# A four-block transformer layer on one core: a finer order of the attention's side work, one shared-expert batch earlier, and a mixture-of-experts dispatch by a table

## The reference

```
x = x + transformer_block(layernorm(x), ctx)   # masked self-attention, LN, cross-attention on ctx, LN, FFN 256-1024-256 (ReLU), LN
x = x + int8_matmul(layernorm(x))              # each row scaled by its amax/127, rounded, times int8 weights
x = x + attention(layernorm(x), ctx, ctx)      # cross-attention, no mask
h = layernorm(x)
logits = h @ router.T ; top 2 of 16 experts, gate = sigmoid(logit)
x = x + sum_k gate_k * down[e_k](silu(gate[e_k](h)) * up[e_k](h)) + shared_down(silu(shared_gate(h)) * shared_up(h))
```

## Time and profile before

| | us |
|---|---|
| median of 3 timed runs | 1551.65 (1545.44 to 1557.75) |
| the profiled execution | 1535.08 |
| its span, first to last instruction | 1533.3 |
| TensorE busy in it | 1291.2 (84%) |
| VectorE busy | 929.4 (61%) |
| ScalarE busy | 671.0 (44%) |
| Pool busy | 466.3 (30%) |

### The profile page before, as it was taken

One profiled execution on the slowest core, in us unless ns is written; L12 is line 12 of the kernel. 1 busy time (PEld: TensorE's weight loads), 2 busy tenths in 40 slices (PEclk: granted clock), 3 DMA queues, 4 the chain that ended last, 5 costly groups with the idle time before them and its releaser, 6 DMA issues. The chain is left out here.

```text
span 1533.3 us, 17810 instructions
## 1 busy us (share of the span) xinstructions
PE 1291.2 (84%) x5544; PEld 562.0 (37%) x5544; DVE 929.4 (61%) x2123; ACT 671.0 (44%) x1243; POOL 466.3 (30%) x728
## 2 busy tenths in 40 slices
PE   5787878878788889988988988988889848999991
PEld 2221322322323233443442443443333224656661
DVE  5799989899885665456455555558667322233333
ACT  1255545455454556445445545535546521112220
POOL 4341633322212323243343343232301004413341
PEclk9598988999899999989999988998989678999996
DMA  7642422424432542221221221222331129722225
GB/s 229 197 131 71 130 77 76 131 56 147 119 92 86 138 125 56 91 69 35 83 77 35 83 76 35 83 68 85 104 89 37 43 73 353 243 71 84 79 64 165
DMA packets 130703, 156.69 MB, mean 102 GB/s; under 512 B 15534, under 2 KB 106162, under 8 KB 130355
## 3 DMA queue, kind: packets, MB, share of 16 engines
q1 hardware_dynamic: 118067, 134.53, 30.0%
q10 hardware_dynamic: 8704, 12.58, 2.6%
q0 software_dynamic: 3840, 8.43, 1.5%
HBM read 93.92 MB, written 63.05 MB: 102 GB/s over the span
## 5 line engine op out<-in xcount | busy, mean ns | idle before, releaser
L1077 DVE TENSOR_REDUCE Mx<-bank 128x1 f32<-128x512 f32 x512 | 341.3, 685 | 304.7 <-PE bank L843 301.4
L750 ACT ACTIVATE prob<-bank 128x512 f32<-128x512 f32 x512 | 290.0, 593 | 253.5 <-PE bank L860 251.8
L860 PE MATMUL bank<-QS,KS 99*128 99x512 bf16 x768 | 315.1, 412 | 68.1 <-ACT prob L750 29.9
L843 PE MATMUL bank<-KS,QS 96*128 96x512 bf16 x768 | 319.2, 416 | 60.1 <-DVE Mx L1074 29.8
L750 ACT ACTIVATE prob<-prob 128x512 f32<-128x512 f32 x256 | 160.6, 629 | 178.5 <-DVE prob L1088 176.8
L873 PE MATMUL bank<-prob,V 128*17 128x512 f32 x1536 | 227.6, 668 | 0.7 <-ACT prob L750 0.7
L860 PEld LDWEIGHTS bank<-QS,KS 99*128 99x128 bf16 x768 | 76.1, 100 | 296.8 <-ACT prob L750 140.2
L843 PEld LDWEIGHTS bank<-KS,QS 96*128 96x128 bf16 x768 | 77.0, 100 | 282.1 <-DVE Mx L1074 104.8
L597 POOL TENSOR_SCALAR MR<-neg 16x128 bf16<-16x128 f32 x48 | 13.8, 288 | 318.5 <-ACT neg L724 318.4
L1088 DVE TENSOR_TENSOR prob<-bank,ff_h 128x512 f32<-128x512 f32 x128 | 87.5, 684 | 16.7 <-PE bank L860 16.3
L1088 DVE TENSOR_TENSOR prob<-bank,mask 128x512 f32<-128x512 f32 x128 | 87.7, 685 | 13.0 <-PE bank L860 12.8
(11 more groups left out here) (157 smaller groups left out, 1727.9 us busy)
## 6 DMA issues: line engine op xcount, KB each, us to landing
stack_scr<-parts SPq DMA_DIRECT2D x48, 384.0 KB, 2.6
QS<-stack_scr SPq DMA_DIRECT2D x48, 384.0 KB, 4.1
KS<-stack_scr SPq DMA_DIRECT2D x48, 384.0 KB, 5.0
stack_scr<-parts SPq DMA_DIRECT2D x48, 256.0 KB, 2.9
w_gu<-in_gate_up ACTq DMA_DIRECT2D x16, 512.0 KB, 5.5
disp<-zero SPq DMA_DIRECT2D x2, 3096.0 KB, 15.4
xr<-disp SPq DMA_DIRECT2D x48, 129.0 KB, 2.0
stack_scr<-parts SPq DMA_DIRECT2D x48, 128.0 KB, 2.8
```

Source lines behind the costliest of these rows:

```text
L750: act.activation(prob[:, U % NP_, j, :], src, ACT.Exp, scale=CAST).then_inc(exp_done, 1)
L843: pe.matmul(bankS[i % NS][:, :], QS[0:STACK, v, qt * P:(qt + 1) * P], KS[0:STACK, v, :], start=True, stop=True).then_inc(s_full, 1)
L860: pe.matmul(bankT[e % NT][:, :], KS[0:ROWS, h, kt * P:(kt + 1) * P], QS[0:ROWS, h, :], start=True, stop=True).then_inc(t_full, 1)
L1077: dve.tensor_reduce(dst, b, AX.X, ALU.max).then_inc(s_read, 1)
```

## The change

1. `batch_order()`: a third list, `at`, is keyed by quarters (`place(step, ...)` takes fractions of a step). Nearly all side work of attentions 4 to 11 moves to it. ScalarE's reading gets names of its own (`head`, `hT`, `aT`, `relu`), placed a quarter step or so behind the product; `turn` and `attT` are single halves, `apply` single rows (`quarters`), `ff2` pieces of four of eight k blocks, `norm` single rows. `oT` and its reading (`merge`) stand at quarters 1 and 3 of the step. The second half of k and q and the values go from five steps ahead of their attention to around its start. The sum of x and the normed rows goes from Pool (`norm`) to VectorE (`stats` 4).
2. The shared expert of batch 0 (`gate`, `up`, `swish`, `hid`, `down`, `sadd`) is done behind the last attention, in phase one (EARLY_SHARED = 1); the shared weights are loaded in phase one, into the mask's place.
3. `acc` (which R now is), `identf` and the transposed rows of batches 1 to 3 stay on chip between the phases; `x_scr`, `tT_scr`, `route_scr` and `disp` go.
4. Dispatch: in place of rows, a pair (row number, gate) is scattered to `tag_scr`, which has 2048 places per expert and is filled with NOWHERE before. 24 such scatters run on Pool in phase one (`dispatch`), 8 at the start of phase two. One gather then reads the 48 tiles' pairs into `table`, TensorE turns it, VectorE makes addresses (`addresses`), and Pool gathers the rows of each tile from `t_scr` by an indirect DMA.
5. Expert weights are issued by SP at the start of phase two; the last reads of `y_tok` (now k-major) are shared between SP and ScalarE.

```diff
+    def place(step, *ops, apart=0):
+        for i, op in enumerate(ops):
+            at.setdefault(round(HG * step) + apart * i, []).append(op)
+    def column(step, n, what, m, lag=0.5):
+        place(step, ("col", n, what, m))
+        place(step + 0.25, ("head", n, what, m))
+        place(step + lag, ("cut", n, what, m))
+    def turned(step, p, i):
+        place(step, *halves("turn", p, i), apart=1)
+        place(step + 0.25, *halves("hT", p, i), apart=1)
+    def attended(e, n, i):
+        p = n % B
+        place(e - 0.5, *halves("attT", n), apart=1)
+        place(e - 0.25, *halves("aT", n), apart=1)
+        place(e + 0.25, *halves("out", n), apart=2)
+        place(e + 0.75, *halves("add", n), apart=2)
+        place(e + 1.5, *halves("stats", p, i), apart=1)
+        place(e + 2.25, *quarters("apply", p, i), apart=1)
...
-            put(late, e, ("attT", n - B), *halves("out", n - B))
-            put(early, e + 1, *halves("add", n - B), *halves("stats", p, a))
-            put(early, e + 2, *halves("apply", p, a), *halves("affine", p, a))
-            put(late, e + 4, ("turn", p, a), *halves("res", p, a))
...
+            attended(e, n - B, a)
+            place(e + 3.75, *halves("affine", p, a), apart=1)
+            turned(e + 5.25, p, a)
+            place(e + 5.75, *halves("res", p, a), apart=1)
+            place(first - 11, ("ctx", n))
+            column(first - 8.75, n, "k", 0)
+            column(first - 6.75, n, "q", 0)
+            column(first - 1.75, n, "k", 1, 1.5)
+            column(first + 0.75, n, "q", 1, 0.75)
...
+                for i, step in enumerate((1, 1.5, 2.25, 2.75, 3.25, 3.75, 4.25, 4.75)):
+                    place(f + step, ("ff1", p, i))
+                    place(f + step + 0.25, ("relu", p, i))
+                for i, step in enumerate((5.75, 6.25, 6.75, 7.75, 8.25, 8.75, 9.25, 9.75)):
+                    place(f + step, ("ff2", p, i // 4, i // 2 % 2, i % 2))
...
+            attended(e, n, 6)
+            turned(e + 3.25, p, 6)
+            place(e + 4.25, ("logits", p))
+            place(e + 4.5, ("top", p))
+            place(e + 5, ("rank", p))
+            place(e + 5.25, ("route", p))
+            if n < NB - 1:
+                for t in range(QT):
+                    place(e + 6.5 + t, ("dispatch", p, t))
+            else:
+                for m, step in enumerate((1, 2.25, 4.5, 5.5)):
+                    place(e + step, ("gate", 0, m), ("up", 0, m))
+                for m, step in enumerate((1.5, 3, 5, 6)):
+                    place(e + step, ("swish", 0, m))
...
+                    place(e + 6.25 + half / 2, ("down", 0, half, 0), ("down", 0, half, 1))
...
             order += between[len(between) * j // HG:len(between) * (j + 1) // HG]
+            order += at.get(HG * step + j, [])
...
-                for half in range(2):
-                    t, x_half = T[p][:, 2 * half:2 * half + 2, :], R[p][:, 2 * half:2 * half + 2, :]
...
-                        pool.tensor_tensor(x_half, x_half, t, ALU.add).then_inc(norm_ready, 1)
...
+                def dispatch(p, t):
+                    pool.wait_ge(route_ready[p], 1)
+                    pool.wait_ge(blanked, 16)
+                    for k in range(2):
+                        pool.indirect_dma_start(tag_scr, bass.IndirectOffsetOnAxis(slot[:, p * QT + t, k:k + 1], 0),
+                                                tags[:, p * QT + t, k, :], None).then_inc(tagged, 16)
...
-                for t in (2 * half, 2 * half + 1):
-                    ins = act.activation(dst[:, t, :], src[:, t, :], ACT.Identity,
...
+                    if i == 4:
+                        link(dve.tensor_tensor(R[p][:, rows, :], R[p][:, rows, :], T[p][:, rows, :], ALU.add))
...
+                def rows(s):
+                    if s >= NX:
+                        pool.wait_ge(xT_full, s - NX + 1)
+                    pool.indirect_dma_start(xr[:, s % NX, :], None, tokens_of,
+                                            bass.IndirectOffsetOnAxis(token[:, s:s + 1], 0)).then_inc(xr_in[s % NX], 16)
+                for s in range(NX):
+                    rows(s)
                 for s in range(TILES):
...
+                    if s + NX < TILES:
+                        rows(s + NX)
...
+                for t in range(1, TT, 2):
+                    act.dma_start(got[:, t % NR, :, :], y[t]).then_inc(got_in[t % NR], 16)
...
+                        if n == 2 * QT - 1:
+                            pe.wait_ge(token_ready, 1)
...
+                        if c == 1 and m == 1:
+                            turn_table()
```

More of the change, by code:

```diff
@@ L90, in batch_order @@
             for half in range(2):
[L91 to L109 removed]
+                step = (s + 3 if p == 0 else first - 5) + half
@@ L110, in batch_order @@
             for half in range(2):
-                put(late, first - 5 + half, ("v", n, half))
-                put(early, first - 4 + half, ("val", n, half))
+                place(first - 0.25 + 1.5 * half, ("v", n, half))
+                place(first + 0.25 + 1.5 * half, ("val", n, half))
             if a == 2:
[L114 to L117, removed]
@@ new lines, in batch_order @@
+                for i, step in enumerate((5.75, 6.25, 6.75, 7.75, 8.25, 8.75, 9.25, 9.75)):
+                    place(f + step, ("ff2", p, i // 4, i // 2 % 2, i % 2))
+                place(f + 8.25, ("ffadd", p, 0))
+                place(f + 10.25, ("ffadd", p, 1), ("again", p))
+                place(f + 10.5, *halves("stats", p, 3), apart=1)
+                place(f + 11.5, *quarters("apply", p, 3), apart=1)
+                for t, step in enumerate((12.5, 13, 13.25, 13.5)):
+                    place(f + step, ("norm", p, t))
@@ L135, in batch_order @@
+                place(f + 19.5, ("i8", p))
+                place(f + 20, *halves("i8add", p), apart=1)
+                place(f + 20.5, *halves("stats", p, 5), apart=1)
+                place(f + 21.5, *quarters("apply", p, 5), apart=1)
+                turned(f + 22.5, p, 5)
+                place(f + 23, *halves("res", p, 5), apart=1)
         for g in range(NG):
             if n or g >= 2:
-                s = first - 1
+                s = first - (2 if n else 1)
                 if n:
@@ L186, in jobs_made @@
 def jobs_made(kind, *at):
[L188 to L191 removed]
     if kind == "i8":
         return [(kind, *at, half) for half in range(2)]
[L194 removed]
+    if kind in ("turn", "attT", "col", "v", "out", "ff1", "i8T", "logits", "rank", "gate", "up"):
         return [(kind, *at)]
[L196 to L200 removed]
+    if kind in ("ff2", "down"):
+        return [(kind, *at[0:2])] if not any(at[2:]) else []
+    if kind in ("max", "oT"):
+        return [(kind, *at)]
     return []
 def jobs_read(kind, *at):
[L206 to L207 removed]
+    read_by_act = {"hT": "turn", "aT": "attT", "relu": "ff1", "swish": "gate"}
+    if kind in read_by_act:
+        return "act", jobs_made(read_by_act[kind], *at)
     made = {"val": "v", "cut": "col", "i8turned": "i8T", "top": "logits", "route": "rank"}
@@ L940, in _ @@
                         read_done(pe, ("ff1", p, FT - 1))
-                        tokens(("ff2", *at[0:2]), at[1], ff_h, w_ff2, FT, (at[2],))
+                        tokens(("ff2", *at[0:2]), at[1], ff_h, w_ff2, FT, (at[2],),
+                               range(FT // 2 * at[3], FT // 2 * (at[3] + 1)))
+                    elif kind in ("gate", "up"):
+                        read_done(pe, ("turn", p, NORMS - 1, KD - 1))
+                        if at == [0, 0]:
+                            pe.wait_ge(shared_in, 48)
+                        columns((kind, *at), s_gu[:, ("gate", "up").index(kind), :, :], hT[p], at[1])
+                    elif kind == "down":
+                        read_done(pe, ("up", p, HT - 1))
+                        tokens(("down", *at[0:2]), at[1], hid[p], s_dn, HT, (at[2],))
                     elif kind == "i8T":
```

553 lines of the change are left out of this document (280 added, 273 removed).

## The result

The changed kernel takes 1483.2 us (median of 4 runs, 1478.0 to 1486.7) beside 1549.6 us before: ratio 0.956, 95% interval 0.951 to 0.962. The forecast was 1479. The total is right; several terms in it are not, and two of them only appear in the experiments.

The account below looks back on a forecast made before the run. VectorE was taken to bound the masked attentions and TensorE the eight unmasked ones. Order -48, masked stretch -4, tail and shared expert -22, dispatch +1 sum to -73 us: 1551.65 - 73 = 1479 us, range 1435 to 1535.

Parts of the forecast that it names:

- Order, -48: Unmasked attentions: the quarter-step order saves 48 us: 8 from filled steps, 20 of waits, 20 of clock.
- rival (a): Attentions: the order gives nothing, waits move to VectorE's maxima or root and apply; 1531 us, chance 0.13.
- Readers come a quarter step behind their product, so most of the 29.9 us should go.: Unmasked attentions: with ScalarE's readers later, TensorE's 29.9 us of waits for exponentials shrink by two thirds, 20 us.
- Late columns, 0: Second half of k and q and values nearer their attention: nothing; a few us per batch if SP's queue is held.
- Masked stretch, -4: Masked attentions, bound by VectorE: the finer order of the next attentions' norms and projections saves 4 us (0 to 15).
- Tail and shared expert, -22: Behind the last attention: one batch's shared expert fills TensorE's idle time in the tail, saving 22 us (15 to 25).
- Dispatch, +1: Start of phase two: table of places by small scatters and a gather is tight, costing 1 us (0 to 5).
- Loop, 0: Expert loop: tiles stay at TensorE's 3.02 us, Pool's scatter and gather needing 2.6 us; no change, little room.
- (c): Expert loop: each Pool issue waits for one VectorE operation, 3.3 us a tile, 14 us more, 1493 us; chance 0.04.
- (d): Expert loop: scatters land late behind gathers in Pool's one queue; 1533 us, or 1591 us at worst; chance 0.08.
- (e): Second phase: weights or table not in time, saved shared work becomes a wait; up to +20 us, 1499 us; chance 0.04.
- rival (b): Attentions: the order recovers 95 us; 1432 us, chance 0.09.

Follow-up runs that it names:

- e1: Changed kernel with the step order of the kernel before for all attentions; tail, table and on-chip data stay: 1525.7 us, ratio 0.984.
- e7: Changed kernel with ScalarE's readers (column heads, ReLUs, copies of turned rows) back in their product's quarter: 1446.8 us, ratio 0.937.
- e8: Changed kernel with k and q of the second half and the values placed ahead of the attention again: 1512.0 us, ratio 0.980.
- e12: e10 with VectorE's readers sooner: every cut a quarter behind its product, each value a quarter sooner: 1488.0 us, ratio 0.963.
- e5: Changed kernel with the turn of the normalised inputs of batches 1 to 3, and their columns, one step later: 1474.4 us, ratio 0.952.
- e13: Changed kernel with only the copies of turned rows back in their product's quarter; ReLUs and column heads stay later: 1451.6 us, ratio 0.943.
- e10: Changed kernel with the edits of e7 and e5 together: 1446.8 us, ratio 0.936.
- e2: Changed kernel with the shared expert of all four batches in the second phase, none in the tail: 1498.2 us, ratio 0.966.
- e9: Changed kernel with each row gather of the expert loop issued twice, the second into an unread buffer: 1509.4 us, ratio 0.979.
- e3: Changed kernel with the loads of the shared expert's weights issued 27 steps later: 1484.7 us, ratio 0.958.
- e6: e5 with the tag scatters of the first batch four steps later: 1473.3 us, ratio 0.953.
- e11: e10 with each batch's eight tag scatters in one piece right behind a load of the rows MR: 1449.7 us, ratio 0.938.

## Why the prediction came out right, point by point

- **Order, -48.** Measured 43 us (e1), inside its bounds, but made of other parts. I had 20 us of waits, 20 of clock and 8 of filled steps. In the unmasked stretch it is 36 us of clock and 7 of idle. My reason for the clock was that long stalls become shorter. Counted in the timelines of TensorE, it idled for more than 2 us seven times in this stretch before, eleven times in e1 and three times in the changed kernel, with nearly the same idle time in all; that fits, but no run separates it from the rest. One reading under it was off: the window at clock 0.51 stands ahead of the 2.47 us stall. What precedes it is a wait of 1.97 us for ScalarE's copy at 669.75 and then three of 0.5 to 1.0 us for VectorE's maxima, the last of them:

```profile
680.24 0.61 PE L843 MATMUL bank<-KS,QS 96*128 96x512 bf16 x1 [1.04 <-DVE Mx L1077]
```

  The waits for exponentials did go, and others took their place, much as rival (a) had it, though for banks and rows more than for the maxima (21.7 to 24.7 us).
- **"Readers come a quarter step behind their product, so most of the 29.9 us should go."** The row was right and the step from it was wrong. Those waits fell by 22 us, of which the later readers gave 3.5 and the placing of the steps the rest; and the readers' delay costs 30 us (e7), because I priced the wait of one engine and not the banks and the turned rows that the others need. The step that failed is that I took ScalarE's waits for the cause of TensorE's: in e7 ScalarE waits 43.0 us ahead of the ReLUs and TensorE still only 10.9 for the exponentials.
- **Late columns, 0.** Mis-sized worst: some 30 us with the packing that hangs on them (e8), where I had 0, and 8 for filled steps. The condition that I named, SP's queue held up in front of the load, is real, though what held it was a write and not a load: up to 41 us in e12. "A few us" a batch was 5 us for each of eight attentions.
- **Masked stretch, -4.** It was +9.9. I had looked at the next attentions' work and not at the inputs' norm, whose apply was cut in four with the turn left behind it (e5: 9.4 us back). The copies cost there as well (e13: 9.4 us back with the inputs' turn unchanged). Together the two give 18.4 us (e10), more than was lost.
- **Tail and shared expert, -22.** The windows give 19.9. My layout counted one batch as free in the tail; by e2 it costs 8.9 there, and what no longer stands at the change of phase pays 6.5 of it back. The out projection took 6.18 us and not 3.72, on a cold clock, in this execution and in e2; in e7 the same tail is 35.0 us (1169.5 to 1204.48). The window of the shared expert is 66.0 us, TensorE busy 63.4 in it, where I had 62.
- **Dispatch, +1.** Right: TensorE turns the table at 1272.10 us with no idle time before it. The margin was thinner than laid out: the last scatter's issue ends at 1255.4 us and the gather starts at 1263.77, so Pool waits 8.4 us for the landing where I had 5.6; the gather lands 6.6 us later, at 1270.4, which leaves 1.7 us. What I did not have is the hole of 6 to 10 us that the scatters make in phase one.
- **Loop, 0.** Right, 3.02 us, with Pool's pair at 2.6 of 3.02 us. (c) and (d) are out: nothing in Pool's issues stretches beside VectorE's copies (mean 1012 ns, 0.3 us between), at up to three issues a tile in e9. The rule that I had weighed from the Trainium skill (SBUF — State Buffer, section "SBUF: two separate sides") is not seen here, but this is no test of it: the page names, as what locks the shared ports, a float32 copy from SBUF to SBUF, and VectorE's three operations in this loop all read PSUM. My sentence that the row "does not agree" with the page said too much. That Pool's issues would bound the loop if there were one more is shown by e9.
- **End, 0.** -1.4 us. **(e)** no wait for weights or table.
- **Sum.** Between the two profiles: start -1.3, masked +9.9, unmasked -35.6, tail and shared expert -19.9, loop and end -1.4, together -48.3 us. The medians differ by 66, because the profiled execution of before ran 14.5 us below its median and that of after 3.5 above; in which stretch the other 18 us lie can't be read from one profile. That the forecast of 73 lies so near to 66 is in good part luck: late columns (some 30 us that I had not counted), readers (some 30 the other way) and the masked stretch (14 us the other way, in part the same microseconds as the readers') cancelled.

The fastest kernel measured is e10 (or e7, the same within the interval): 0.936 of the kernel before, 0.979 of the changed one. That is 0.0475, some 73 us, better than the old order in the new kernel (e1), between my 48 and the 95 of rival (b).

## What to carry to other kernels

A wait is a cost only on the engine that sets the end: before moving a reader away from its product, ask who needs the bank, or the row, that it gives back. Where banks are dealt out by the order of one list, moving a reader also changes which bank every product behind it gets; print that table before and after. Where one list orders all queues, an operation that moves past a load moves its DMA past it as well; compare the queues, not the engines. And when a piece is cut finer, whatever stands behind its last part has to move too.

## What the runs showed of the hardware

- The gain of an order can be nearly all clock: 3235 matmuls took 699.7 us at a granted mean of 0.92 and 663.8 at 0.97, with 7 us of idle time between them; the means of whole runs do not overlap (0.913 to 0.926 in e1, 0.935 to 0.947 in the changed kernel). It can be all idle time too: e13 has the same 664 us busy and 20.5 less idle. What decides this is not settled here.
- Scatters of 128 pairs of 8 bytes take Pool 0.96 us each, and the last was waited for 8.4 us after its issue, beside the loads of the expert weights. A load of the rows MR, three DMAs of 4 KB, issued among them was awaited for 6.1 to 9.6 us in ten kernels of the new order; in the unmasked attentions of the old order (e1) no such wait passed 3.5 us, and before the change none passed 3.7. In e3 no packet is seen between 1041 and 1045 us, the last 4 us of that wait. That it takes the two in flight together is borne out by e6 and e11; by what they hold each other is open.
